# A weight split of expert 1 moved from VectorE to POOL in a routed feed-forward kernel

## The reference, cut to what matters

```python
router_logits = xf @ w_gate.T
routing_weights = softmax_integer(router_logits)
top_w, top_i = jax.lax.top_k(routing_weights, _TOP_K)
...
for e in range(E):
    h = jax.nn.silu(xf @ w1[e].T) * (xf @ w3[e].T)
    out = out + combine[:, e:e + 1] * (h @ w2[e].T)
return out.reshape(orig_shape)
```

## Time and profile before

| | |
|---|---|
| median of 3 runs | 202.05 us (201.3 to 202.57) |
| profiled execution | 201.05 us, of which the span from first to last instruction is 199.3 us |
| PE busy | 192.5 us (97% of the span) |
| POOL busy | 130.3 us (65%) |
| DVE busy | 108.2 us (54%) |
| ACT busy | 82.5 us (41%) |

### The profile page before, as it was taken

How to read it: one execution, slowest core, us unless ns; L and a number is a source line. 1 busy time by engine, 2 the same in 40 slices (tenths; PEclk the granted TensorE clock), 3 DMA queues, 4 the chain that set the end, 5 groups by cost and what they waited for, 6 DMA issues and landing times.

```text
span 199.3 us, 3883 instructions
## 1 busy us (share of the span) xinstructions
PE 192.5 (97%) x1209; PEld 169.6 (85%) x1209; DVE 108.2 (54%) x308; ACT 82.5 (41%) x225; POOL 130.3 (65%) x116
## 2 busy tenths in 40 slices
PE   7998999989999999999999999999999999999992
PEld 6677998778899888989988998899889889988861
DVE  0777898874545644435443553345675435543673
ACT  3756583587643323432333333234323333332740
POOL 8300008569898699999999999998544455418500
PEclk9999999999999999999999999999999999999998
DMA  4999522999993114183364356007312111101915
GB/s 130 348 378 386 189 105 68 333 356 361 359 361 117 58 53 132 48 277 99 109 201 169 109 192 189 13 3 250 120 54 54 54 61 60 67 30 53 358 41 212
DMA packets 14419, 32.67 MB, mean 164 GB/s; under 512 B 2400, under 2 KB 7648, under 8 KB 14272
## 3 DMA queue, kind: packets, MB, share of 16 engines
q1 hardware_dynamic: 11008, 25.70, 37.9%
q0 software_dynamic: 2128, 5.64, 8.8%
q10 hardware_dynamic: 1264, 1.07, 1.6%
HBM read 25.45 MB, written 6.96 MB: 163 GB/s over the span
## 4 chain that ended last, share of the span: by engine, by line
PE 86%; DMA 5%; DVE 4%; issue 1%; SPq 1%; ACT 1%; ACTq 0%; DVEq 0%; POOL 0%; POOLq 0%
PE gu L1210 27%; PE gu L1219 14%; PE ya L1247 7%; PE ht L1226 7%; PE ya L1248 6%; PE ya L1249 6%; DMA rows<-expert_rows 4%; PE ya L1018 3%; PE xt L1188 2%; PE gu L1076 2%; DMA expert_rows<-rows,dst_i 1%; PE ya L1242 1%; PE ya L1241 1%; PE gu L1264 1%; PE ya L1170 1%
## 5 line engine op out<-in xcount | busy, mean ns | idle before, releaser
L1210 PE MATMUL gu<-w_all,xs_hi 128*128 (+2 forms) x276 | 70.7, 377 | 0.3 <-issue 0.3
L890 DVE TENSOR_TENSOR hid<-gu,sg 128x256 f32<-128x256 f32 x46 | 19.5, 424 | 62.2 <-ACT sg L613 62.1
L1210 PEld LDWEIGHTS gu<-w_all,xs_hi 128*128 128x128 f32 x276 | 46.7, 188 | 4.8 <-issue 0.5
L613 ACT ACTIVATE sg<-gu 128x256 f32<-128x256 f32 x46 | 17.7, 385 | 73.2 <-PE gu L1219 73.2
L466 POOL TENSOR_TENSOR w_all<-raw,w_all 128x1024 fp32r<-128x1024 f32 (+2 forms) x14 | 43.9, 3147 | 3.8 <-DVE w_all L872 3.7
L460 POOL DMA_INDIRECT rows<-cond_rows,src_i x22 | 24.4, 1109 | 27.4 <-DVE src_i L835 22.9
L1219 PE MATMUL gu<-w_all,xs_lo 128*128 (+1 forms) x138 | 40.5, 375 | 0.0
L1247 PE MATMUL ya<-w_all,h_hi 128*128 (+1 forms) x115 | 38.4, 334 | 0.6 <-DVE rows L911 0.5
L482 POOL DMA_INDIRECT expert_rows<-rows,dst_i x21 | 20.3, 965 | 22.8 <-DVE hid L890 12.0
L1248 PE MATMUL ya<-w_all,h_hi 128*128 (+1 forms) x115 | 32.5, 283 | 0.0
L1249 PE MATMUL ya<-w_all,h_lo 128*128 (+1 forms) x115 | 32.3, 281 | 0.0
(11 more groups left out here) (192 smaller groups left out, 260.7 us busy)
## 6 DMA issues: line engine op xcount, KB each, us to landing
raw<-expert_weights SPq DMA_DIRECT2D x6, 896.0 KB, 4.8
raw<-expert_weights SPq DMA_DIRECT2D x6, 640.0 KB
raw<-expert_weights SPq DMA_DIRECT2D x6, 512.0 KB, 4.8
expert_rows<-zeros SPq DMA_DIRECT2D x1, 2048.0 KB, 14.4
rows<-expert_rows SPq DMA_DIRECT2D x4, 512.0 KB, 5.3
x<-x_t SPq DMA_DIRECT2D x4, 256.0 KB, 4.6
cond_rows<-c_rows ACTq DMA_DIRECT2D x4, 256.0 KB, 2.1
raw<-x_t SPq DMA_DIRECT2D x1, 1024.0 KB, 4.9
```

Of the source, the lines that this page charges most:

```text
L890: nc.vector.tensor_tensor(hid[i % HBUFS][:, :].rearrange("p (a b) -> p a b", b=P), bank[:, :].rearrange("p (a k b) -> p a k b", k=2, b=P)[ ...
L1210: nc.tensor.matmul(out, stay_hi[:, kc * P:(kc + 1) * P], moving(at, part + first + kc * P, n), start=kc == 0 and part == HI_COLS, stop=False)
```

## The change

DVE no longer subtracts expert 1's third piece and tail in item 3. POOL does it with its own helpers, after its first five gathers and ahead of expert 2. It waits for ACT's copy of the piece and for expert 0's count first, and then, as before, for its own count of expert 1.

```diff
@@ -487,7 +487,12 @@
                 if FETCHED[e][0] + n < FETCHED[e][1]:
                     gather(FETCHED[e][0] + n)
 
-            pool.wait_ge(w_ready, 2)
+            pool.wait_ge(whi_ready, len(PIECES) * (STAGED + 1))
+            pool.wait_ge(w_ready, STAGED)
+            low(STAGED, 2)
+            tail_low(STAGED).then_inc(w_ready, 1)
+
+            pool.wait_ge(w_ready, STAGED + 1)
             for e in (2, 3):
                 for k in range(len(PIECES) - 1):
                     pool.wait_ge(whi_ready, len(PIECES) * e + k + 1)
@@ -991,8 +996,6 @@
                     second_lo(4).then_inc(second_ready, 1)
                 if i == 3:
                     destinations()
-                    expert_lo(1, 2)
-                    expert_tail_lo(1).then_inc(w_ready, 1)
                 if i in SHARED_AT:
                     expert_lo(SHARED_AT[i], 2).then_inc(third_ready, 1)
                 if i >= 4 and j == 1:
```

## The result

The changed kernel takes 206.6 us as a median (206.44 to 208.0), the kernel before 202.03 us. By the medians that is 4.6 us slower. The ratio measured is 1.0253, with a 95% interval from 1.0215 to 1.0291, which is 5.1 us (4.3 to 5.9). The forecast was 205.0 us, in a range up to 206.0. The direction and the stall were as forecast; the time lies outside the range.

What follows compares the result with a forecast made beforehand. The prediction took PE, busy 97% of the span, as the bound. DVE's `destinations()`, shut out by POOL, would delay a down matmul by 2.97 us: 202.05 + 2.97 = 205.0 us, range 201.2 to 206.0 us.

Steps and rivals of the forecast that it cites:

- the stall: First down matmul of slot 1 on PE: starts at 46.15 instead of 43.18, a loss of 2.97 us.
- POOL's own work: POOL's added subtraction (2.94 us from 37.96) and tail (0.74 us): expert 1 whole at 41.6, hidden with 0.9 us to spare.
- The shut-out: `destinations()` on DVE: held for each POOL instruction it meets, until 44.22; likeliest case, chance 0.55, 205.0 us.
- all steps one POOL instruction later: Variant of the shut-out: if L842 is held as well, L846 is the one that meets expert 2.
- the path chosen: L844 held to 40.90, L846 to 41.73, L850 (41.83) behind expert 2's first piece (41.82), so DVE shut out until 44.22.
- One reading: DVE instruction on SBUF alone: stretched from 0.19 to 0.32 us in one case beside a scatter.
- The clock: Rival "a worse stall": PE clock falls to 1.2 GHz for half an item, 1.1 us more, 206 us; chance 0.05.
- nothing on PE gives it back: End of the sum: PE has no other idle time there, so the whole 2.97 us loss stays.
- the difference to the median: Median of the runs shown lies 1.0 us above the profiled execution, so 204.0 us became 205.0 us.
- No shut-out: Rival: POOL lets DVE's short instructions through, PE's stall goes, gain 0.65 us, 201.4 us; chance 0.25.
- L850 ahead of expert 2: Rival: L850 gets its turn before expert 2's first piece, loss 0.55 us, 202.6 us; chance 0.15.

Runs made afterwards that it cites:

- its table: Kernel before with an extra POOL table of row numbers (writes SBUF only), only the pair `spare`, `dst_i` left in item 3, the rest in item 8: 201.76 us, ratio 0.9981.
- the filler run: Changed kernel plus twelve matmuls of zeros into a free PSUM bank, as work for PE in the stall: 205.05 us, ratio 1.017.
- the taken-apart version: Changed kernel with only the two-input pair of `destinations()` left in item 3, the others in item 8: 206.27, 207.66, 206.4 and 202.85 us.
- the table against `destinations()`: Kernel before with an extra POOL table of row numbers (writes SBUF only) ahead of its wait for expert 1: 203.16 us, ratio 1.0068.

## Why the prediction was wrong

**POOL's own work: right.** The subtraction was forecast from 37.96 with 2.94 us and ran from 38.21 with 2.96 us. Expert 1 was whole at 41.87, hidden as forecast, and no wait of PE for weights came.

**The shut-out: right, with a wrong detail.** Read from the lengths of gathers, it was forecast that a DVE instruction waits for POOL's to end and then has its turn. It waits, but it has no turn between the two POOL subtractions that run back to back (the tail starts at 41.12, the first one ends at 41.17): it was held through both, to 41.9. The gather's turn between two DVE instructions had suggested otherwise. The forecast named this variant (all steps one POOL instruction later), and it leads to the same end, since both paths meet expert 2's first piece. That the path chosen met it too was in part luck: by the forecast's sum POOL was ahead by 0.01 us there. The two holds were forecast to end with it at 44.22 and did at 44.30.

One reading was wrong and carried no price: of the two instructions of the earlier trace rows, the one called not stretched (0.19 us, at 140.06) lay beside a scatter too (139.74 to 140.70), so these rows show no stretching by POOL.

**The stall: right.** Down matmul forecast at 46.15, measured at 46.05; loss forecast 2.97 us, measured 2.87 us, of which 0.10 us lie ahead of the change (item 3's product at 38.59 instead of 38.49).

The Trainium skill, page "SBUF — State Buffer", section "Who interferes with whom", states that a VectorE instruction with two SBUF inputs contends with a GpSimd instruction that reads SBUF and not with one that only writes it. The traces agree: `spare` took 2.49 us beside POOL's subtractions and 0.17 us beside its table. The same section of the Trainium skill states that `tensor_scalar` can run in a two-port mode, when its operands meet the conditions for it, and that an instruction in that mode contends with GpSimd. The one-input `tensor_scalar` was held by both kinds of POOL instruction (2.62 and 1.26 us), which agrees; no run shows in which mode it ran.

**The clock: the step that failed.** The sum ended with "nothing on PE gives it back", and with nothing more on top. A fall of the clock was a rival of its own, with a chance of 0.05 and half an item, 1.1 us. It came, and cost 1.55 us: six down matmuls and one item's gate and up ran mostly at 1.2 GHz. The mean granted clock of the span was 0.982 to 0.988 in all four runs, against 0.997 in the first profile of the kernel before. The 1.55 us are from one trace; two of the four runs have the lower means, 0.982 and 0.983, and may have lost more. With this term the sum is 202.03 + 2.87 + 1.55 = 206.45 us; without it the forecast's 205.0 is what the filler run gave, 205.05. The rival was also sized too small: its 206.1 us lay at the upper end of the range, which left no room for a fall that lasts longer than half an item.

A row that pointed to it stood there: the granted clock fell in the only stretch where PE stopped for long. The mean of 0.89 hides when it fell, though. In the kernel before PE's last matmul ends at 195.57, and a finer window shows the clock at its upper level until about 198.1:

```profile
198.00:199.00 1.00, 0.00 (x0) 0.00 (x0) 0.00 (x0) 0.00 (x0) 0.00 (x0) 0.54 0.44 164
```

So the row showed the clock falling after PE had stopped, with no work behind it. What such a fall costs PE when work follows could not be read there.

**The reading of one profile.** The first profile lay 1.0 us under the median, and the second one suggests why: a stall of ACT, worth 1.25 us of PE's time there, was missing in it. Taking the difference to the median, as the forecast did, was right.

**The rivals.** No shut-out: fell. L850 ahead of expert 2: fell for this kernel; one run of the taken-apart version at 202.85 us is what such a win would look like.

## What to carry to other kernels

Before moving elementwise work to POOL, list what DVE does in that time: an instruction on SBUF alone, however short (24 columns here), can wait for the whole POOL instruction, and the one that is chained behind it for the next. Price a PE standstill like this one, 2.3 us and soon after it 0.7 us, with the work behind it at half clock, and look whether a short DVE step can be moved elsewhere first: here that alone won 0.36% (0.21% to 0.51%), about as much as the change could have won at most (0.71 us).

## What the runs showed that was not expected

A waiting DVE instruction isn't let in between two POOL instructions that run back to back: it waited 2.65 us through both, and in every profile with POOL's split and `destinations()` or a part of it in item 3 it is the same. The clock fell not in the standstill (1.00 up to 46.0) but after PE had resumed, and stayed at 0.50 for 3.4 us while PE was fully busy; with standstills of 0.22 and 0.75 us, or of 0.49 and 0.75 us (the table against `destinations()`), it stayed at 1.00. ACT stands still once for 3.4 to 3.8 us, up to a point between 142 and 148 us, in eleven of the twelve profiles, and PE loses 1.1 to 1.3 us to it in the two worked out above.
